# Norms between sublayers: ScalarE copies the residual stream, and halves of the rows go over two engines

## The chip, the core and the metric

The kernel runs on one core of one Trainium2 chip. The metric is the device time of one execution in microseconds (us), lower is better; shown is the median of three runs. The engines are TensorE (PE in the profile, its weight loads PEld), VectorE (DVE), ScalarE (ACT), GpSimd (POOL) and SyncE (SP), which issues nearly all DMAs. Each works through its own queue in order and meets the others by semaphores.

## The reference

A residual stream `x` of 128 rows by 512 columns (float32) goes through eight sublayers. Each is fed the layer norm of the stream, without gain or offset, and its result is added to the stream:

```python
def _layernorm(x, axis=-1, eps=1e-05):
    m = jnp.mean(x, axis=axis, keepdims=True)
    v = jnp.var(x, axis=axis, keepdims=True)
    return (x - m) / jnp.sqrt(v + eps)
...
x = x + _L0_gnn_ref(_layernorm(x, axis=-1), edge_index, L0_gnn_W, L0_gnn_a)
...
x = x + _L3_gnn_ref(_layernorm(x, axis=-1), edge_index, L3_gnn_W1, L3_gnn_b1, ...)
x = x + _L3_ffn_ref(_layernorm(x, axis=-1)[None], L3_ffn_router_w, L3_ffn_router_b, ...)[0]
```

The sublayers, numbered from 0 as their norms are: 0 graph attention over the edges, 1 grouped-query attention with a routed choice of weights, 2 a graph layer with linear attention (performer), 3 a product-key memory (it picks the best 16 of 256 sums for each row and head), 4 attention over the edges (exphormer), 5 eight transformer experts behind a gate, 6 three graph convolutions, 7 eight LSTM-like experts behind a router.

## The kernel before

Everything stays in on-chip memory, one row of the stream to a partition; weights come in by DMA ahead of use or, for the experts, as soon as the order of the experts is known. Every engine has one hand-written queue, and a step waits on a named semaphore's count; the order of the work is this writing, no planner is at work. Semaphores are named in `sig(...)` and waited for in `at(name, value)`. On VectorE, `settle()` drains the engine's own queue before a result is read again. `ps` is the accumulator memory that TensorE writes, eight banks of 512 columns.

A norm takes these steps; k is its number.

- The sums. At norms 2, 3, 4, 5 and 7, TensorE adds the residual stream and the sublayer's result in the accumulator memory, in two halves of 256 columns (norms 2, 4, 7) or four quarters of 128 (norms 3, 5), each signalled by `residual_summed`. At norms 0, 1 and 6 the stream lies in `x` already.
- Statistics on VectorE: `residual_norm` (L1907 to L1924) takes bn_stats of each part and aggregates; `layer_norm` (L1880) does it from `x` and serves norms 0 and 6; `layer_norm_routed` (L1891) serves norm 1, where the centred rows are written first because sublayer 1's choice needs them.
- GpSimd: `layer_norm_rstd` (L659 to L661) raises the variance to the power -1/2, `ln_rstd`.
- Rows on VectorE: two instructions, one for each half, write `y`, each signalled by `y_ready` (L1888, L1902, L1920). In `residual_norm` two copies from the accumulator memory to `x` follow (L1923), the second signalled by `x_updated`.
- TensorE: `layer_norm_transpose` (L1086 to L1093) waits for a half of `y` and transposes its two chunks of 128 columns into bank 7 or 6, signalled by `y_transposed`.
- ScalarE: `layer_norm_t` (L755 to L760) copies both halves of the transposed rows to `y_t`; the second copy is signalled by `y_t_ready`.
- TensorE waits for `y_t_ready` and `x_updated` and begins the sublayer's first product over the four chunks of `y_t`: mostly `project_t` (L1104 to L1109), four chunks summed for each output block; in sublayer 5 the gate's scores (L1663), in 6 the first convolution (L1721), in 7 the router's scores in bank 6 (L1829).

Ahead of a norm's transposes TensorE runs `keep_clock` (L1080 to L1084), products of the identity that nobody reads: 7 or 9 of them, 26 ahead of norm 6.

Behind norm 0 VectorE turns the edges to floats (L1985 to L1987) and makes the two one-hot tables (L1990) from which TensorE counts edges (L1197), and then copies attention terms (L1996). Behind norm 2 it spreads `y_t` into `x1_t`; behind norm 6 it adds a bias to `x` (L2509). GpSimd waits for `y_ready` of norm 5 before it adds `y` to expert rows (L722, L715).

Of the kernel before, what the change touches and what calls it, by code (L numbers as in the profile page):

```python
# [22 lines left out]
ALU = mybir.AluOpType  # L23
# [10 lines left out]
SUBLAYERS = 8  # L34

# [135 lines left out]
def build(nc, A, out):  # L171
# [14 lines left out]
    with ctx:  # L186
# [452 lines left out]
        def _(pool):  # L639
# [82 lines left out]
            pool.wait_ge(*at("y_ready", 12))  # L722
# [27 lines left out]
        def _(act):  # L750
# [58 lines left out]

            layer_norm_t(2)  # L810
# [35 lines left out]

            layer_norm_t(3)
# [30 lines left out]

            layer_norm_t(4)
# [9 lines left out]

            layer_norm_t(5)  # L890
# [114 lines left out]

            layer_norm_t(7)
# [69 lines left out]
        def _(pe):  # L1076
# [9 lines left out]
            def layer_norm_transpose(k):  # L1086

                for half in range(2):
                    pe.wait_ge(*at("y_ready", 2 * k + half + 1))
# [3 lines left out]
                    last.then_inc(sig("y_transposed"), 1)  # L1093
# [84 lines left out]
            pe.wait_ge(*at("y_t_ready", 1))  # L1178
            gat_w = slot("l0_W").rearrange("p (m c n) -> p m c n", m=CH, c=CH)
            pe.wait_ge(*at("gat_w_first_landed", 16))  # L1180
            for m in range(CH):
                if m == 2:
                    weights("l0_W")
                for c in range(CH):
                    last = pe.matmul(ps[:, m // 2, m % 2 * P:(m % 2 + 1) * P], gat_w[:, m, c, :], y_t[:, c, :],  # L1185
# [60 lines left out]
            pe.wait_ge(*at("y_t_ready", 2))  # L1246
# [36 lines left out]
            pe.wait_ge(*at("y_t_ready", 3))  # L1283
# [3 lines left out]
            for c in range(CH):  # L1287
                for w, name in enumerate(("perf_wq", "perf_wk")):
# [93 lines left out]
            pe.wait_ge(*at("y_t_ready", 4))  # L1382
# [3 lines left out]
            project_t(0, y_t, matrix("peer_wq"), chunks=2).then_inc(sig("peer_q_projected"), 1)  # L1386
# [57 lines left out]
            pe.wait_ge(*at("y_t_ready", 5))  # L1444
            pe.wait_ge(*at("x_updated", 4))
            weights("exph_wq")
            project_t(0, y_t, matrix("exph_wq")).then_inc(sig("exph_q_projected"), 1)
# [32 lines left out]
            pe.wait_ge(*at("y_t_ready", 6))  # L1480
# [181 lines left out]
            for c in range(CH):  # L1662
# [1058 lines left out]
```

## Time and profile before

| what | value |
|---|---|
| timed runs | 450.26, 448.14, 447.12 us; median 448.14 |
| profiled execution, span | 449.3 us (the page gives no time of its own beside the span) |
| TensorE busy | 412.4 us, 92% |
| VectorE busy | 214.4 us, 48% |
| ScalarE busy | 120.0 us, 27% |
| GpSimd busy | 35.0 us, 8% |
| mean granted TensorE clock | 0.981 |
| HBM read | 103.82 MB, 232 GB/s over the span |

The profile is of one execution, from its first to its last instruction, the span. Start times are us from the span's start, single durations us or ns. A group `out<-in` names what an instruction writes and reads; L1084 is a line of the kernel, and a line can be that of a helper, so that one line serves all norms. One float32 product of 128 by 128 by 128 appears as two records. TensorE's share of busy time includes `keep_clock`. The granted clock of 1.00 is 2.4 GHz, 0.50 is 1.2 GHz.

### The profile page before, as it was taken

How to read it: one execution, taken by the hardware profiler on the slowest of the kernel's cores; microseconds unless marked ns; L12 is line 12 of the kernel's file. 1: busy time of each engine (PE TensorE's matmuls, PEld its weight loads, DVE VectorE, ACT ScalarE, POOL GpSimd, SP SyncE). 2: the span in 40 equal slices, each digit the busy share in tenths (PEclk: the TensorE clock that was granted, in tenths of full speed). 3: DMA queues.
4: the chain of work that ended last, by engine and by line, in shares of the span. 5: the costliest groups of instructions: out<-in, count | busy, mean ns of one | idle time of the engine just before them, and what ended most of it. 6: DMA issues, size and time to landing. Idle time of an engine off the chain costs nothing.

```text
span 449.3 us, 7597 instructions
## 1 busy us (share of the span) xinstructions
PE 412.4 (92%) x2819; PEld 308.1 (69%) x2819; DVE 214.4 (48%) x631; ACT 120.0 (27%) x347; POOL 35.0 (8%) x68
## 2 busy tenths in 40 slices
PE   7998999994748989999998999999999999999996
PEld 6698655883247878797784668756778896394492
DVE  6744464457994254462754527557442631111102
ACT  2322313303220102251531325442111332222121
POOL 4000010011232001001000010002010000000000
PEclk9999999998699999999999899999999999999999
DMA  8999579222002200899999999336300299999900
GB/s 274 402 422 338 223 292 388 93 95 93 0 2 91 97 0 3 338 395 423 418 295 304 355 423 288 90 117 274 131 0 0 85 427 421 419 422 421 415 12 24
DMA packets 19631, 104.57 MB, mean 233 GB/s; under 512 B 3550, under 2 KB 5470, under 8 KB 7946
## 3 DMA queue, kind: packets, MB, share of 16 engines
q1 hardware_dynamic: 19306, 104.07, 60.9%
q8 instruction: 22, 0.36, 0.3%
q14 instruction: 15, 0.12, 0.1%
q10 hardware_dynamic: 288, 0.02, 0.0%
HBM read 103.82 MB, written 0.26 MB: 232 GB/s over the span
## 4 chain that ended last, share of the span: by engine, by line
PE 64%; DVE 15%; issue 7%; DMA 6%; ACT 3%; POOL 2%; DVEq 1%; SPq 1%; POOLq 0%; ACTq 0%
PE ps L1108 12%; PE ps L1096 8%; PE ps L1770 6%; PE ps L1510 5%; DMA dense<-in_l_w 5%; PE ps L1490 3%; PE ps L1499 3%; PE ps L1593 2%; PE ps L1084 2%; PE ps L1252 2%; PE ps L1092 1%; DMA ew<-in_l_wq 1%; PE ps L1185 1%; PE ps L1835 1%; PE ps L1289 1%
## 5 line engine op out<-in xcount | busy, mean ns | idle before, releaser
L1084 PE MATMUL ps<-ident 128*128 128x128 f32 x372 | 48.4, 284 | 2.7 <-POOL ident L647 2.7
L1084 PEld LDWEIGHTS ps<-ident 128*128 128x128 f32 x372 | 46.0, 199 | 5.1 <-POOL ident L647 2.7
L1108 PEld LDWEIGHTS ps<-y_t,ew 128*128 128x128 f32 x352 | 39.9, 192 | 1.7 <-issue 1.7
L1108 PE MATMUL ps<-y_t,ew 128*128 128x128 f32 x352 | 40.2, 275 | 0.0
L1096 PE MATMUL ps<-ew,y_t 128*128 128x512 f32 x72 | 32.7, 597 | 0.0
L1510 PE MATMUL ps<-y_t,ew 128*128 128x128 f32 x224 | 27.5, 277 | 0.0
L1510 PEld LDWEIGHTS ps<-y_t,ew 128*128 128x128 f32 x224 | 26.1, 192 | 0.8 <-issue 0.7
L768 ACT ACTIVATE prob_store<-ps,nmax_s 128x128 f32<-128x128 f32 x56 | 19.7, 384 | 14.6 <-DVE nmax_s L1957 14.6
L1096 PEld LDWEIGHTS ps<-ew,y_t 128*128 128x128 f32 x72 | 13.0, 190 | 13.5 <-issue 13.3
L758 ACT COPY y_t<-ps 128x256 f32<-128x256 f32 x16 | 5.7, 373 | 61.5 <-PE ps L1092 61.1
L2561 DVE SCALAR_TENSOR_TENSOR t<-prob_store 128x512 f32<-128x512 f32 x6 | 4.2, 692 | 36.4 <-ACT prob_store L1018 20.4
L720 POOL TENSOR_TENSOR ln_rstd<-ln_mv,minus_half 128x1 f32<-128x1 f32 x12 | 6.6, 547 | 133.3 <-DVE ln_mv L2321 133.3
L1499 PE MATMUL ps<-y_t,ew 128*128 128x128 f32 x128 | 15.7, 278 | 0.2 <-DMA ew<-in_l_wq 0.2
L1499 PEld LDWEIGHTS ps<-y_t,ew 128*128 128x128 f32 x128 | 14.9, 192 | 0.8 <-DMA ew<-in_l_wq 0.4
L1593 PE MATMUL ps<-ew,ctx_t 128*128 128x256 f32 x64 | 14.6, 381 | 0.3 <-ACT ctx_t L915 0.3
L1408 PE MATMUL ps<-dense,eq_t 128*8 128x512 f32 x8 | 6.4, 968 | 8.1 <-ACT big L866 8.1
L1593 PEld LDWEIGHTS ps<-ew,ctx_t 128*128 128x128 f32 x64 | 11.8, 190 | 1.9 <-ACT ctx_t L915 0.5
L768 ACT ACTIVATION_READ_ACCUMULATOR prob_store<-ps,nmax_s 128x1 f32 x56 | 12.5, 224 | 0.0
L1108 PE MATMUL ps<-y_t,dense 128*128 128x128 f32 x96 | 11.2, 277 | 0.9 <-ACT y_t L758 0.9
L1108 PEld LDWEIGHTS ps<-y_t,dense 128*128 128x128 f32 x96 | 10.9, 192 | 1.4 <-ACT y_t L758 1.4
L1096 PE MATMUL ps<-ew,x_t 128*128 128x512 f32 x24 | 11.1, 596 | 0.0
L1955 DVE TENSOR_REDUCE nmax<-ps 128x4 f32<-128x512 f32 x14 | 9.6, 686 | 2.5 <-PE ps L1119 2.3
(514 smaller groups left out, 751.0 us busy)
## 6 DMA issues: line engine op xcount, KB each, us to landing
ew<-in_l_w SPq DMA_DIRECT2D x20, 1024.0 KB, 21.8
dense<-in_l_w SPq DMA_DIRECT2D x12, 1024.0 KB, 21.2
ew<-in_l_wv SPq DMA_DIRECT2D x8, 1024.0 KB, 13.8
ew<-in_l_wk SPq DMA_DIRECT2D x7, 1024.0 KB, 16.3
ew<-in_l_wq SPq DMA_DIRECT2D x6, 1024.0 KB, 12.0
erows<-in_l_rows SPq DMA_DIRECT2D x4, 1280.0 KB, 12.5
ew<-in_l_wo SPq DMA_DIRECT2D x5, 1024.0 KB, 14.8
ew<-in_gqa_wq SPq DMA_DIRECT2D x3, 1024.0 KB, 10.9
```

What stands on the lines that cost most here:

```text
L720: pool.tensor_tensor(ln_rstd[:], ln_mv[:, 1:2], minus_half[:, 0:1], ALU.pow).then_inc(sig("l2_rstd_ready"), 1)
L768: last = nc.scalar.activation(prob[:, s, :], ps[:, 3 + a, g * P:(g + 1) * P], ACT.Exp, bias=nmax_s[:, s:s + 1], scale=scale, accum_out=rsu ...
L1084: pe.matmul(ps[:, b, 3 * P:4 * P], ident[:], ident[:], start=True, stop=True)
L1096: return pe.matmul(bank(b), in_t[:, c, :], w[:, c, :], start=(c == 0), stop=(c == CH - 1))
L1108: last = pe.matmul(ps[:, b, m * n:(m + 1) * n], w[:, c, (first + m) * P:(first + m + 1) * P], in_t[:, c, 0:n], start=(c == 0), stop=(c == ...
L1252: last = pe.matmul(ps[:, b, m * P:(m + 1) * P], w[:, m, c, :], y_t[:, c, :], start=(c == 0), stop=(c == CH - 1))
L1490: last = pe.matmul(ps[r, b, 0:columns.stop - columns.start], in_t[:, c, r], w_of[:, c, columns], start=(c == 0 and not started), stop=(c = ...
L1499: last = pe.matmul(ps[:, 0, m * P:(m + 1) * P], l2_w("q", p)[:, c, m * P:(m + 1) * P], y_t[:, c, :], start=(c == 0), stop=(c == CH - 1))
L1510: last = pe.matmul(ps[:, 1, m * P:(m + 1) * P], l2_w("k", p)[:, c, m * P:(m + 1) * P], y_t[:, c, :], start=(c == 0), stop=(c == CH - 1))
L1593: last = pe.matmul(ps[:, 5 + half, 0:D // 2], ctx_t[:, c, :], l2_w("o", L2_STEPS[t][0])[:, c, columns], start=(c == 0), stop=(c == CH - 1))
L1770: last = pe.matmul(ps[cols_of, b, :], in_t[:, c, cols_of], w_of[:, c, :], start=(c == 0 and not started), stop=(c == CH - 1))
L1955: dve.tensor_reduce(nmax[:, s], bank_chunks(3 + a), AX.X, ALU.max, negate=True)
```

## The change

The norms 0 and 2 to 7 (all but 1) are split by halves over two engines, and the first product waits by halves.

- ScalarE, no longer VectorE, copies the residual stream from the accumulator memory to `x` (`residual_copies`), each half as soon as VectorE has signalled its statistics (`residual_counted`). The two copies signal `x_copied` and `x_updated`.
- VectorE's `split_norm` subtracts the mean from the left half of `x` without waiting for `ln_rstd` (`y_centred`), and then makes the right half as before, but from `x`. ScalarE multiplies the left half by `ln_rstd` in place.
- The transposed left half is copied by ScalarE, the right one by VectorE (`second_half_t`, which stands right behind the norm in VectorE's queue). At norm 1 ScalarE copies both.
- TensorE waits for the first half of `y_t` ahead of chunk 0 of the first product and for the second ahead of chunk 2 (`normalised_chunk`).
- The semaphores `y_ready`, `y_transposed` and `y_t_ready` become one for each half. In sublayer 7 the router's scores and counts go to bank 5 and the transposed gates to bank 6, in exchange, since VectorE may still be reading bank 6.

The diff, cut: the same edits at other norms are left out.

```diff
+NORMS_OF_ROWS = tuple(range(SUBLAYERS))
+
+SPLIT_NORMS = tuple(k for k in NORMS_OF_ROWS if k != 1)
+
+RESIDUAL_NORMS = (2, 3, 4, 5, 7)
...
-            pool.wait_ge(*at("y_ready", 12))
+            pool.wait_ge(*at("y_ready0", 6))
+            pool.wait_ge(*at("y_ready1", 6))
...
             def layer_norm_t(k):
-                for half in range(2):
-                    act.wait_ge(*at("y_transposed", 2 * k + half + 1))
-                    last = nc.scalar.copy(y_t[:, 2 * half:2 * half + 2, :].rearrange("p c n -> p (c n)"),
-                                          ps[:, 7 - half, 0:2 * P])
-                last.then_inc(sig("y_t_ready"), 1)
+                n = NORMS_OF_ROWS.index(k) + 1
+                if k in SPLIT_NORMS:
+                    act.wait_ge(*at("y_centred", SPLIT_NORMS.index(k) + 1))
+                    act.wait_ge(*at("ln_rstd_ready", k + 1))
+                    nc.scalar.mul(y[:, 0:D // 2], y[:, 0:D // 2], ln_rstd[:]).then_inc(sig("y_ready0"), 1)
+                for half in range(1 if k in SPLIT_NORMS else 2):
+                    act.wait_ge(*at(f"y_transposed{half}", n))
+                    nc.scalar.copy(y_t[:, 2 * half:2 * half + 2, :].rearrange("p c n -> p (c n)"), ps[:, 7 - half, 0:2 * P]) \
+                        .then_inc(sig(f"y_t_ready{half}"), 1)
+
+            def residual_copies(summed, parts, halves):
+
+                for half, src in enumerate(halves):
+                    act.wait_ge(*at("residual_counted", summed + parts * (half + 1) // 2))
+                    out_half = x[:, half * D // 2:(half + 1) * D // 2]
+                    nc.scalar.copy(out_half if parts == 2 else out_half.rearrange("p (b n) -> p b n", b=2), src) \
+                        .then_inc(sig(("x_copied", "x_updated")[half]), 1)
...
+            residual_copies(0, 2, residual_halves((2, 3)))
             layer_norm_t(2)
...
+            residual_copies(2, 4, [ps[:, 0:2, 0:P], ps[:, 2:5:2, 0:P]])
             layer_norm_t(3)
...
             def layer_norm_transpose(k):
 
                 for half in range(2):
-                    pe.wait_ge(*at("y_ready", 2 * k + half + 1))
+                    pe.wait_ge(*at(f"y_ready{half}", NORMS_OF_ROWS.index(k) + 1))
                     for c in range(2):
                         f = (2 * half + c) * P
                         last = pe.transpose(ps[:, 7 - half, c * P:(c + 1) * P], y[:, f:f + P], ident[:])
-                    last.then_inc(sig("y_transposed"), 1)
+                    last.then_inc(sig(f"y_transposed{half}"), 1)
+
+            def normalised_chunk(k, c):
+
+                if c % 2 == 0:
+                    pe.wait_ge(*at(f"y_t_ready{c // 2}", NORMS_OF_ROWS.index(k) + 1))
...
-            def project_t(b, in_t, w, chunks=CH, first=0, n=P):
+            def project_t(b, in_t, w, chunks=CH, first=0, n=P, norm=None):
 
                 for m in range(chunks):
                     for c in range(CH):
+                        if norm is not None and m == 0:
+                            normalised_chunk(norm, c)
...
-            pe.wait_ge(*at("y_t_ready", 4))
             pe.wait_ge(*at("x_updated", 3))
             weights("peer_wq")
 
-            project_t(0, y_t, matrix("peer_wq"), chunks=2).then_inc(sig("peer_q_projected"), 1)
+            project_t(0, y_t, matrix("peer_wq"), chunks=2, norm=3).then_inc(sig("peer_q_projected"), 1)
...
-                last = pe.matmul(ps[:, 6, 0:E], y_t[:, c, :], router_w[:, c, :], start=(c == 0), stop=(c == CH - 1))
+                normalised_chunk(7, c)
+                last = pe.matmul(ps[:, 5, 0:E], y_t[:, c, :], router_w[:, c, :], start=(c == 0), stop=(c == CH - 1))
...
+            def split_norm(k):
+
+                left, right = slice(0, D // 2), slice(D // 2, D)
+                settle()
+                if k in RESIDUAL_NORMS:
+                    dve.wait_ge(*at("x_copied", RESIDUAL_NORMS.index(k) + 1))
+                dve.tensor_scalar(y[:, left], x[:, left], ln_mv[:, 0:1], None, ALU.subtract).then_inc(sig("y_centred"), 1)
+                if k in RESIDUAL_NORMS:
+                    dve.wait_ge(*at("x_updated", k))
+                dve.wait_ge(*at("ln_rstd_ready", k + 1))
+                dve.tensor_scalar(y[:, right], x[:, right], ln_mv[:, 0:1], ln_rstd[:], ALU.subtract, ALU.mult) \
+                    .then_inc(sig("y_ready1"), 1)
+
+            def second_half_t(k):
+                dve.wait_ge(*at("y_transposed1", NORMS_OF_ROWS.index(k) + 1))
+                dve.tensor_copy(y_t[:, 2:4, :].rearrange("p c n -> p (c n)"), ps[:, 6, 0:2 * P]).then_inc(sig("y_t_ready1"), 1)
...
             def layer_norm(k):
                 settle()
                 dve.bn_stats(ln_st[:, 0:6], x[:])
                 settle()
                 dve.bn_aggr(ln_mv[:], ln_st[:]).then_inc(sig("ln_var_ready"), 1)
+                split_norm(k)
...
-            def residual_norm(k, summed, parts, halves):
+            def residual_norm(k, summed, parts):
 
                 stats = half_st if len(parts) == 2 else part_st
                 for n, part in enumerate(parts):
                     dve.wait_ge(*at("residual_summed", summed + n + 1))
-                    dve.bn_stats(stats[:, 6 * n:6 * n + 6], part)
+                    dve.bn_stats(stats[:, 6 * n:6 * n + 6], part).then_inc(sig("residual_counted"), 1)
                 settle()
                 dve.bn_aggr(ln_mv[:], stats[:]).then_inc(sig("ln_var_ready"), 1)
-                settle()
-                dve.wait_ge(*at("ln_rstd_ready", k + 1))
-                shaped = lambda tile, half, src: tile[:, half * D // 2:(half + 1) * D // 2] if len(src.shape) == 2 else \
-                    tile[:, half * D // 2:(half + 1) * D // 2].rearrange("p (b n) -> p b n", b=2)
-                for half, src in enumerate(halves):
-                    dve.tensor_scalar(shaped(y, half, src), src, ln_mv[:, 0:1], ln_rstd[:], ALU.subtract, ALU.mult) \
-                        .then_inc(sig("y_ready"), 1)
-                for half, src in enumerate(halves):
-                    last = dve.tensor_copy(shaped(x, half, src), src)
-                last.then_inc(sig("x_updated"), 1)
+                split_norm(k)
...
             layer_norm(0)
+            second_half_t(0)
...
-            residual_norm(2, 0, residual_halves((2, 3)), residual_halves((2, 3)))
-
-            dve.wait_ge(*at("y_t_ready", 3))
+            residual_norm(2, 0, residual_halves((2, 3)))
+            second_half_t(2)
+
+            dve.wait_ge(*at("y_t_ready0", 3))
+            settle()
```

## Rows read from the trace of the kernel before

**Rows 1.** The page's chain that ended last: shares of the span by engine.

```profile
PE 64%; DVE 15%; issue 7%; DMA 6%; ACT 3%; POOL 2%; DVEq 1%; SPq 1%; POOLq 0%; ACTq 0%
```

**Rows 2.** Chain of waits in order of time, norm 4 and before: start, us, what.

```profile
137.51 1.79 PE ps L1084 x16
...
139.98 1.58 PE ps L1436 x6
...
141.58 0.86 DVE half_st L1912 x2
...
142.82 0.59 POOL ln_rstd L661
...
143.43 0.56 DVE y L1920
...
144.03 0.44 PE ps L1092 x2
...
144.49 0.45 PE ps L1092 x2
...
144.96 0.38 ACT y_t L758
```

**Rows 3.** Timeline of norm 4: start, us, engine, line, operation; idle time and releaser in brackets.

```profile
144.34 0.75 DVE L1923 COPY x<-ps 128x256 f32<-128x256 f32 x2
...
144.51 0.82 ACT L758 COPY y_t<-ps 128x256 f32<-128x256 f32 x2 [9.45 <-PE ps L1092]
...
145.38 3.84 PE L1108 MATMUL ps<-y_t,dense 128*128 128x128 f32 x32 [0.46 <-ACT y_t L758]
```

**Rows 4.** Chain of waits in order of time, behind norm 5.

```profile
180.24 4.83 DMA ew<-in_l_wq
```

**Rows 5.** Groups by shape: form and count, busy us, mean ns, idle before.

```profile
L866 ACT ACTIVATE big<-big,negbest 128x256 f32<-128x256 f32 x8 | 4.1, 508 | 0.3
...
L786 ACT ACTIVATE t<-ctxv,small 128x512 f32<-128x512 f32 x1 | 0.7, 722 | 2.8 <-DVE small L2032 2.8
...
L1923 DVE COPY x<-ps 128x256 f32<-128x256 f32 x10 | 3.7, 414 | 0.0
...
L1888 DVE TENSOR_SCALAR y<-x,ln_mv,ln_rstd 128x256 f32<-128x256 f32 x4 | 1.5, 417 | 1.8 <-POOL ln_rstd L661 1.8
...
L1902 DVE TENSOR_SCALAR y<-t,ln_rstd 128x256 f32<-128x256 f32 x2 | 0.6, 350 | 0.1
```

**Rows 6.** Timeline of norm 6.

```profile
330.60 0.69 ACT L758 COPY y_t<-ps 128x256 f32<-128x256 f32 x2 [6.20 <-PE ps L1092]
...
331.34 1.99 PE L1721 MATMUL ps<-dense,y_t 128*128 128x256 f32 x8 [0.46 <-ACT y_t L758]
```

**Rows 7.** Timeline of norm 1.

```profile
29.23 0.55 POOL L661 TENSOR_TENSOR ln_rstd<-ln_mv,minus_half 128x1 f32<-128x1 f32 x1 [23.54 <-DVE ln_mv L1896]
29.25 0.49 DVE L1898 TENSOR_SCALAR t<-x,ln_mv 128x512 f32<-128x512 f32 x1
```

**Rows 8.** Timeline of norm 0 and of the edge tables.

```profile
6.38 0.17 DVE L1985 CAST src_f<-src_i 128x17 f32<-128x17 int32 x1
...
6.67 0.89 PE L1092 MATMUL ps<-ident,y 128*128 128x128 f32 x4
...
7.34 0.65 ACT L758 COPY y_t<-ps 128x256 f32<-128x256 f32 x2 [4.33 <-PE ps L1092]
...
9.17 2.42 DVE L1990 TENSOR_TENSOR ew<-iota_f,dst_f 128x2176 bf16<-128x2176 f32 x1
...
13.03 0.28 DVE L1996 COPY gat_l<-ps 8x128 f32<-8x128 f32 x1 [1.44 <-PE ps L1193]
```

**Rows 9.** Timeline of TensorE alone, end of the product-key stage.

```profile
133.42 1.94 PE L1429 MATMUL ps<-x_t,prob_store 128*128 128x128 f32 x8 [5.19 <-POOL x_t L691]
```

**Rows 10.** Stretches: busy us of PE, PEld, DVE, ACT, POOL, then granted clock, DMA share, GB/s.

```profile
134.00:136.00 2.00, 2.00 (x9) 1.83 (x8) 1.90 (x8) 0.71 (x2) 0.60 (x1) 0.50 0.00 0
...
138.00:140.00 2.00, 1.77 (x17) 1.58 (x15) 0.37 (x2) 0.00 (x0) 0.00 (x0) 1.00 0.00 0
```

More of the change, by code:

```diff
@@ L887, in _ @@
             nc.scalar.copy(heads_v[:, :, 0:DH], bank_heads(2)).then_inc(sig("exph_v_ready"), 1)
+            residual_copies(8, 4, [ps[:, 1 + c:3 + c, 0:P] for c in (0, 2)])
             layer_norm_t(5)
@@ L1245, in _ @@
             keep_clock(1, times=9)
-            pe.wait_ge(*at("y_t_ready", 2))
+            for c in (0, 2):
+                normalised_chunk(1, c)
             def project_copied(b, w, copied):
@@ L1443, in _ @@
             layer_norm_transpose(4)
-            pe.wait_ge(*at("y_t_ready", 5))
             pe.wait_ge(*at("x_updated", 4))
             weights("exph_wq")
-            project_t(0, y_t, matrix("exph_wq")).then_inc(sig("exph_q_projected"), 1)
+            project_t(0, y_t, matrix("exph_wq"), norm=4).then_inc(sig("exph_q_projected"), 1)
             weights("exph_wk")
@@ L1718, in _ @@
                     for c in range(CH):
+                        if k == 0 and half == 0:
+                            normalised_chunk(6, c)
                         if k and half == 0 and c % 2 == 0:
@@ L1841, in _ @@
             pe.wait_ge(*at("lstm_tables_ready", LSTM_TABLES))
-            pe.matmul(ps[:, 6, 8:16], ones[:], mask8, start=True, stop=True)
-            pe.matmul(ps[:, 6, 16:24], upper, mask8, start=True, stop=True).then_inc(sig("router_counted"), 1)
+            pe.matmul(ps[:, 5, 8:16], ones[:], mask8, start=True, stop=True)
+            pe.matmul(ps[:, 5, 16:24], upper, mask8, start=True, stop=True).then_inc(sig("router_counted"), 1)
             first_gate((2, 3)).then_inc(sig("l3_gates_projected"), 1)
@@ L1846, in _ @@
             pe.wait_ge(*at("lstm_gated_ready", 1))
-            pe.transpose(ps[0:E, 5, 0:P], gated[:], ident[:]).then_inc(sig("lstm_gated_transposed"), 1)
+            pe.transpose(ps[0:E, 6, 0:P], gated[:], ident[:]).then_inc(sig("lstm_gated_transposed"), 1)
             lstm_gates(0, (2,))
@@ L1884, in layer_norm @@
                 dve.bn_aggr(ln_mv[:], ln_st[:]).then_inc(sig("ln_var_ready"), 1)
-                settle()
-                dve.wait_ge(*at("ln_rstd_ready", k + 1))
-                for half in (slice(0, D // 2), slice(D // 2, D)):
-                    dve.tensor_scalar(y[:, half], x[:, half], ln_mv[:, 0:1], ln_rstd[:], ALU.subtract, ALU.mult) \
-                        .then_inc(sig("y_ready"), 1)
+                split_norm(k)
             def layer_norm_routed(k):
@@ L1900, in layer_norm_routed @@
                 dve.wait_ge(*at("ln_rstd_ready", k + 1))
-                for half in (slice(0, D // 2), slice(D // 2, D)):
-                    dve.tensor_scalar(y[:, half], t1[:, half], ln_rstd[:], None, ALU.mult).then_inc(sig("y_ready"), 1)
+                for n, half in enumerate((slice(0, D // 2), slice(D // 2, D))):
+                    dve.tensor_scalar(y[:, half], t1[:, half], ln_rstd[:], None, ALU.mult).then_inc(sig(f"y_ready{n}"), 1)
             def residual_halves(banks):
                 return [ps[:, b, 0:D // 2] for b in banks]
-            def residual_norm(k, summed, parts, halves):
+            def residual_norm(k, summed, parts):
                 stats = half_st if len(parts) == 2 else part_st
@@ L2172, in _ @@
             batch_norm(1, ctx_t, N2G, N2B)
-            residual_norm(3, 2, [ps[:, b, 0:P] for b in (0, 1, 2, 4)], [ps[:, 0:2, 0:P], ps[:, 2:5:2, 0:P]])
+            residual_norm(3, 2, [ps[:, b, 0:P] for b in (0, 1, 2, 4)])
+            second_half_t(3)
             dve.wait_ge(*at("peer_q_projected", 1))
@@ L2278, in _ @@
             batch_norm(2, ctx_t, BNG, BNB)
-            residual_norm(5, 8, [ps[:, 1 + c, 0:P] for c in range(CH)], [ps[:, 1 + c:3 + c, 0:P] for c in (0, 2)])
+            residual_norm(5, 8, [ps[:, 1 + c, 0:P] for c in range(CH)])
+            second_half_t(5)
             def top2():
@@ L2532, in _ @@
             dve.wait_ge(*at("router_counted", 1))
-            dve.scalar_tensor_tensor(keys8[:, 1:E], ps[:, 6, 9:16], 8.0, iota_f[:, 1:E], ALU.mult, ALU.subtract)
+            dve.scalar_tensor_tensor(keys8[:, 1:E], ps[:, 5, 9:16], 8.0, iota_f[:, 1:E], ALU.mult, ALU.subtract)
             settle()
```

29 lines of the change are left out of this document (16 added, 13 removed).

## Prediction

> **What bounds the kernel now.** I read the page's chain of waits first: TensorE holds 64% of it, VectorE 15%, ScalarE 3%, GpSimd 2% [rows 1]. So the kernel is one long chain that hops between engines, and what counts is the links that a norm between sublayers puts into it. The chain in order of time shows them for norm 4 [rows 2]: VectorE's statistics end at 142.44, GpSimd's power at 143.41, VectorE writes the first half of y until 143.99, TensorE transposes it from 144.03, and the second half only from 144.49, because VectorE brings it that much later; ScalarE's second copy ends at 145.34. The timeline of the same stretch has the first product at 145.38 [rows 3]: 1.97 us from the power's end to the product, in which TensorE has only four transposes. The same links, within 0.01 us, stand at five places, norms 2, 3, 4, 5 and 7. The timeline also shows what is not among them: VectorE's two copies of x end at 145.09, before y_t is there, and ScalarE had been idle for 9.45 us before its two copies.
>
> Time saved there is passed on. Behind norm 5 comes the order of the experts, and only that sends the load at 180.24, on which TensorE then waits until 185.07 [rows 4]: issue and landing move with the norm, they do not absorb it.
>
> **The change, part by part.** The sums are for the profiled execution: span 449.3, and the page gives no time around it, which I take as the same before and after. The timed runs have a median of 448.14 and a highest of 450.26, so the profile is an ordinary execution 0.3% above the median; I take the differences off the median.
>
> *Halves side by side, and a product that waits by halves (norms 2, 3, 4, 5, 7).* The path after the power becomes: ScalarE multiplies the centred left half by ln_rstd, TensorE transposes it, ScalarE copies it, the product starts. No row has a ScalarE multiply of 128x256 from SBUF with a per-row scale. It should not be under the plain 128x256 copy from PSUM, 0.38 [rows 2], nor over the 128x512 activation with a per-row operand at L786, 0.722 [rows 5]. The nearest row is L866, 128x256 from SBUF with a per-row operand, 0.508: I take 0.51. It starts at 143.43 as VectorE did and ends at 143.94, 0.05 before VectorE's half did (143.99). The first transpose moves to 143.98. ScalarE's first copy began 0.48 after it (144.51 against 144.03 [rows 2, 3]), so it runs from 144.46 to 144.84, and the product starts at 144.88 instead of 145.38. Gain 0.50, nearly all of it the 0.45 by which the second half used to trail. With the multiply's two ends: 0.63 and 0.29.
>
> The right half must not spoil it. VectorE's subtract-and-multiply from SBUF takes 0.417 (L1888 [rows 5]) and ends at 143.85, before ScalarE's, so the four transposes run in one piece. In norm 6, where the halves lay close, the second copy began 0.31 after the first (0.69 for both, 0.38 for one [rows 2, 6]). VectorE's copy of the second half, 0.414 (L1923), would run from 144.77 to 145.18 and let chunk 2 go at 145.22. Chunks 0 and 1 keep TensorE busy until then: 32 records take 3.84 [rows 3], 0.12 each, so their four take 0.48, until 145.36. Cover 0.14; without it the product loses only what is missing.
>
> *The copies of x.* Two of 0.38 on ScalarE, each behind the statistics of its half, beside the aggregation and the power: the second runs from 142.47 to 142.85, 0.56 before the power ends. Queued behind it on ScalarE is only this norm's own work. VectorE's centring of the left half, 0.350 (L1902), starts with the power at 142.82 and ends at 143.17, 0.24 ahead of it. I cost both at nothing; were a copy twice as long, the 0.56 would still hide it. VectorE loses its 0.75 of copies and gains nothing by that: behind them it waits for TensorE's products, in norm 2 for y_t itself.
>
> *A VectorE instruction beside the power.* Norm 1 shows that pair already [rows 7]: the power from 29.23 to 29.78, VectorE's centring of 128x512 from 29.25 to 29.74, and the power, at 0.55, is not longer than norm 4's 0.59 without company. Nothing again. The Trainium skill ("SBUF — State Buffer", Who interferes with whom) says that a VectorE instruction of this kind and a GpSimd one shut each other out for the whole instruction; norm 1's rows do not agree, but a rival below keeps it.
>
> *Norm 6.* x lies in SBUF there, and VectorE needed 0.41 for its first half; ScalarE's 0.51 is 0.10 later. The first copy ends 0.31 before the second did. Gain 0.21 of the wait that ended at 331.34 [rows 6]. The addition to x behind VectorE's new wait is wanted only in the third layer.
>
> *Norm 0, a loss.* VectorE now waits for the second transposes before it turns to the edges, and behind those TensorE waits for the one-hot tables [rows 8]. The transposes stand behind TensorE's fillers and start at 6.67 whatever the norm does; ScalarE's second copy began near 7.61, so VectorE's would run from 7.61 to 8.02, and the casts that began at 6.38 come 1.64 later. The tables ended at 11.59 (9.17 + 2.42) and will end at 13.23; the chain met VectorE at 13.03. So 0.20 is lost, plus 0.03 of start-up: 0.23. TensorE's own gain of 0.27 (one copy instead of two) is overtaken by that. The ends: a gain of 0.27 if the tables had the room, a loss of 1.64 if there were no slack.
>
> *The rest.* Norm 1 keeps its form. GpSimd's wait (both halves instead of a count of 12) guards residual rows off the path. SP's queue is untouched. Router scores in bank 5 instead of 6 are the same instructions.
>
> Sum: 5 x 0.50 + 0.21 - 0.23 = 2.48 us, so 448.14 - 2.48 = 445.7, and a span near 446.8. The multiply at 0.38 and norm 0 a gain of 0.27 make it 3.8 (444.3); the multiply at 0.722 makes it 1.2 (446.9), norm 0's worst end 1.1 (447.1).
>
> **Rivals.**
> *The second half is the late one.* VectorE's copy comes so late that TensorE gains nothing from its early chunks: the product in effect starts at 145.22, a gain of 0.16 each and none in norm 6, 5 x 0.16 - 0.23 = 0.57: 447.6. For it: a cover of only 0.14. Against it: the 0.48 of work is counted from rows, and a late half costs only the difference.
>
> *VectorE and GpSimd hold each other up.* The power begins when the centring ends (143.17 instead of 142.82), or the centring when the power ends; either puts 0.35 on five norms and on norm 6, 2.1 together: 447.8. For it no row speaks; against it norm 1. It is what the skill's rule named above would give.
>
> *The clock comes back too late: slower.* Near the end of the product-key stage TensorE has waited 5.19 us [rows 9]; the granted clock is then 0.50 (1.2 GHz) and from 138 on 1.00 (2.4 GHz) [rows 10]. Behind that the chain still runs 1.79 and 1.58 us on TensorE [rows 2]. Should the clock come back only after these, they double: 3.4 us more, 449.1, slower than before. It decides at 137.5. For it: the stage is entered over a microsecond earlier, and no row says what that does. Against it: the idle time ahead of it is the same.
>
> *The clock comes back sooner.* The eight records at 133.42 took 1.94 [rows 9] at the lower level; with the upper one 0.97 less, and about as much for what follows until 137.5: some 1.8 us, 443.9, and 442.5 with the good ends above.
>
> **How the numbers follow.** The forecast 0.62 (its own range 444.3 to 447.1), the late half 0.12, the mutual hold 0.07, the late clock 0.07, the early clock 0.12. A measurement of this kernel tells about 1% from no change, here 4.5 us: below 443.7, above 452.6. Faster by more needs the early clock and part of the good ends: 0.12 with the forecast's own tail. Slower by more needs the late clock and two more losses: 0.04. That leaves 0.84 within 1%. The range goes from 443.8 to 448.3: it holds the forecast, the late half, the hold and the early clock alone, and leaves out the late clock and the early one with more beside it.
>
> **What would show it.** In the profile of after: the product of norm 4 some 1.47 us after the power's end instead of 1.97, ScalarE's multiply near 0.51, VectorE's copy done before chunk 2 is due, the power still 0.55 to 0.59, the edge casts near 8.0 and the tables' end near 13.2, the granted clock around 137 as before. I am wrong if the product waits for VectorE, if the power grows, if ScalarE's multiply starts well after the power's end, or if the stages behind the norms do not keep their lengths.

## The result and the profile after

In the first set of runs the changed kernel takes 446.31 us (median of 12, 444.98 to 450.1) and the kernel before 449.81 beside it; the ratio is 0.9914, 95% interval 0.9892 to 0.9936. By the medians that is 3.5 us faster, by the ratio 3.9, somewhere between 2.9 and 4.9. A second set, below, gives 0.9941 (0.9900 to 0.9983), 2.7 us by the ratio. Both are under 1%. The forecast was 445.7, a gain of 2.5.

The profiled execution has a span of 445.1 us and was timed at 446.79, so about 1.7 us lie around the span. VectorE's busy time is 1.6 us less than before and ScalarE's 5.1 more. Its engines:

```profile
PE 408.7 (92%) x2819; PEld 308.4 (69%) x2819; DVE 212.8 (48%) x628; ACT 125.1 (28%) x357; POOL 35.2 (8%) x68
```

The timeline of the changed kernel: norm 0 and the edge tables (which answers to [rows 8]), the aggregation of norm 1, norm 4 (which answers to [rows 2, 3]), and norm 6's power and product (to [rows 6]). Columns are start, duration, engine, line, operation; in brackets the idle time before and what ended it.

```profile
6.59 0.60 PE L1119 MATMUL ps<-ident,y 128*128 128x128 f32 x4
...
7.01 0.37 ACT L770 COPY y_t<-ps 128x256 f32<-128x256 f32 x1 [0.69 <-PE ps L1119]
...
7.57 0.17 DVE L2025 CAST src_f<-src_i 128x17 f32<-128x17 int32 x1
...
10.36 2.42 DVE L2030 TENSOR_TENSOR ew<-iota_f,dst_f 128x2176 bf16<-128x2176 f32 x1
...
12.83 0.95 PE L1232 MATMUL ps<-ew 128*128 128x128 bf16 x14 [0.38 <-DVE ew L2030]
...
28.36 0.20 DVE L1944 BATCH_NORM_AGGREGATE ln_mv<-ln_st 128x2 f32<-128x9 f32 x1
...
141.58 0.58 POOL L667 TENSOR_TENSOR ln_rstd<-ln_mv,minus_half 128x1 f32<-128x1 f32 x1 [7.26 <-DVE ln_mv L1962]
141.59 0.35 DVE L1921 TENSOR_SCALAR y<-x,ln_mv 128x256 f32<-128x256 f32 x1
...
142.26 0.51 ACT L767 ACTIVATE y<-y,ln_rstd 128x256 f32<-128x256 f32 x1 [0.67 <-POOL ln_rstd L667]
142.27 0.41 DVE L1925 TENSOR_SCALAR y<-x,ln_mv,ln_rstd 128x256 f32<-128x256 f32 x1 [0.32 <-POOL ln_rstd L667]
...
142.82 0.66 PE L1119 MATMUL ps<-ident,y 128*128 128x128 f32 x4 [0.54 <-ACT y L767]
...
143.29 0.37 ACT L770 COPY y_t<-ps 128x256 f32<-128x256 f32 x1 [0.53 <-PE ps L1119]
143.51 0.42 DVE L1930 COPY y_t<-ps 128x256 f32<-128x256 f32 x1 [0.82 <-PE ps L1119]
...
143.78 0.97 PEld L1142 LDWEIGHTS ps<-y_t,dense 128*128 128x128 f32 x8 [0.54 <-issue]
143.81 1.02 PE L1142 MATMUL ps<-y_t,dense 128*128 128x128 f32 x7 [0.34 <-ACT y_t L770]
...
325.33 0.55 POOL L667 TENSOR_TENSOR ln_rstd<-ln_mv,minus_half 128x1 f32<-128x1 f32 x1 [2.25 <-DVE ln_mv L1936]
...
327.53 1.75 PE L1756 MATMUL ps<-dense,y_t 128*128 128x256 f32 x7 [0.34 <-ACT y_t L770]
```

What to see: ScalarE's multiply, which no row of before had, takes 0.51 us as estimated. The four transposes run in one piece (0.66), the two copies side by side, and the product runs on without waiting for the second. The power is 0.58 long although VectorE's centring lies wholly beside it. But the chain has two cracks. The power ends at 142.16 and the multiply starts 0.10 later; ScalarE's copy ends at 143.66 and the product starts 0.15 later (the load of its weights is put down to "issue", that is, to nothing the profile shows). So the product comes 1.65 us after the power's end, against 1.97 before and a forecast of 1.47. The same holds in norms 2, 3, 5 and 7: 0.33 to 0.35 gained in each, and 0.11 in norm 6 (1.76 before, 1.65 after).

Aligning TensorE's records of the two profiles one by one, the changed kernel is ahead by 0.60 us at norm 1's power, 0.91 at norm 2's product, 1.57 at norm 4's, 1.90 at norm 5's, 3.65 at 249 us, and 4.17 at norm 7's product. Beside the norms there are two sources nobody forecast: 0.6 us before norm 2 and 1.6 us in the experts' stage, between 244 and 250 us. The experiments went after the cracks, the parts of the change, and these two.

### The profile page after: what moved, and what is told of

Same layout as the page of the kernel before. It is cut to its first block, busy times and chain, and to the rows that moved or that the text cites. A ratio compares the mean times of both kernels' runs of the same rounds, so it can differ in the third digit from the quotient of the medians.

```text
span 445.1 us, 7617 instructions
## 1 busy us (share of the span) xinstructions
PE 408.7 (92%) x2819; PEld 308.4 (69%) x2819; DVE 212.8 (48%) x628; ACT 125.1 (28%) x357; POOL 35.2 (8%) x68
## 4 chain that ended last, share of the span: by engine, by line
PE 45%; DMA 6%; issue 5%; DVE 3%; ACT 1%; SPq 1%; DVEq 0%; POOL 0%; POOLq 0%; ACTq 0%
PE ps L1142 9%; PE ps L1804 6%; PE ps L1128 6%; PE ps L1543 5%; DMA dense<-in_l_w 5%; PE ps L1523 3%; PE ps L1532 3%; PE ps L1626 2%; DMA ew<-in_l_wq 1%; PE ps L1870 1%; PE ps L1647 1%; PE ps L1162 1%; PE ps L1111 1%; PE ps L1634 1%; PE ps L1153 1%
## 5 line engine op out<-in xcount | busy, mean ns | idle before, releaser
L1111 PE MATMUL ps<-ident 128*128 128x128 f32 x372 | 50.0, 290 | 2.7 <-POOL ident L653 2.7
L1111 PEld LDWEIGHTS ps<-ident 128*128 128x128 f32 x372 | 47.8, 205 | 5.1 <-POOL ident L653 2.7
L778 ACT COPY x<-ps 128x256 f32<-128x256 f32 x10 | 3.7, 373 | 32.7 <-DVE part_st L1960 18.2
L1443 PE MATMUL ps<-dense,eq_t 128*8 128x512 f32 x8 | 4.9, 772 | 8.1 <-ACT big L890 8.1
```

What stands on the lines that cost most here:

```text
L1111: pe.matmul(ps[:, b, 3 * P:4 * P], ident[:], ident[:], start=True, stop=True)
L1443: last = pe.matmul(ps[0:E, 0, :], eq_t[:, c, :], matrix("gate_wk")[:, c, :], start=(c == 0), stop=(c == CH - 1))
```

## The experiments

**How to compare them.** Single runs of one kernel spread over as much as 5 us. Each timed run lists its span and its mean granted clock, and these go together: within the kernels of this study the span falls by 0.32 us for each 0.001 of mean clock (a straight line fitted by least squares over 197 runs). In the table the last column takes every kernel's mean span to a clock of 0.980 with that slope; the plus-minus is its standard error. The kernel before was run anew with each set of experiments; its three sets give 448.1, 448.0 and 448.0 at 0.980, so kernels of different sets may be compared.

| kernel | runs | mean span, us | mean clock | span at 0.980, us |
|---|---|---|---|---|
| before | 75 | 448.26 | 0.9792 | 448.01 ± 0.12 |
| changed, both sets | 21 | 445.15 | 0.9814 | 445.61 ± 0.25 |
| late_first | 12 | 445.41 | 0.9800 | 445.41 ± 0.33 |
| norm0_whole | 6 | 444.78 | 0.9820 | 445.43 ± 0.30 |
| halves_alone | 12 | 446.78 | 0.9798 | 446.72 ± 0.27 |
| joint | 12 | 447.94 | 0.9814 | 448.40 ± 0.34 |
| one_engine | 12 | 445.57 | 0.9802 | 445.62 ± 0.23 |
| one_engine_late | 12 | 445.96 | 0.9773 | 445.10 ± 0.15 |
| one_engine_best, both sets | 14 | 444.64 | 0.9805 | 444.80 ± 0.21 |
| split_best | 9 | 445.32 | 0.9798 | 445.25 ± 0.22 |
| before_drain | 12 | 448.58 | 0.9796 | 448.44 ± 0.14 |

At equal clock the change is worth 2.4 us (95%: 1.9 to 2.9).

**1. The order of waits (late_first).**

```diff
-                    act.wait_ge(*at("y_centred", SPLIT_NORMS.index(k) + 1))
                     act.wait_ge(*at("ln_rstd_ready", k + 1))
+                    act.wait_ge(*at("y_centred", SPLIT_NORMS.index(k) + 1))
...
             layer_norm_transpose(4)
+            pe.wait_ge(*at("y_t_ready0", 5))
             pe.wait_ge(*at("x_updated", 4))
```

> Edit: the changed kernel, where the wait that ends last is written first of those ahead of an instruction (ln_rstd ahead of y_centred on ScalarE and ahead of the x waits on VectorE, y_t_ready0 ahead of x_updated and the weights on TensorE). In the changed kernel the first product of a norm starts 1.64 us after the power's end, where 1.47 was forecast; 0.07 of the missing time lies between the power's end and ScalarE's multiply (0.10 instead of 0.03), 0.10 between ScalarE's copy and the product (0.14 instead of 0.04). Theory, order of the waits: the lags go back to about 0.04 and 0.05, the product comes 1.44 to 1.50 us after the power, and the kernel is 7 x 0.15 = about 1 us faster than the changed one. Rival, the lags belong to the engines and to two engines waiting on one semaphore: 1.64 as in the changed kernel, and the same time.

The timeline of late_first, norm 4:

```profile
142.65 0.58 POOL L667 TENSOR_TENSOR ln_rstd<-ln_mv,minus_half 128x1 f32<-128x1 f32 x1 [8.08 <-DVE ln_mv L1969]
...
143.26 0.51 ACT L767 ACTIVATE y<-y,ln_rstd 128x256 f32<-128x256 f32 x1 [0.60 <-POOL ln_rstd L667]
...
144.30 0.37 ACT L770 COPY y_t<-ps 128x256 f32<-128x256 f32 x1 [0.53 <-PE ps L1119]
...
144.72 0.52 PEld L1142 LDWEIGHTS ps<-y_t,dense 128*128 128x128 f32 x4 [0.48 <-ACT y_t L770]
144.72 0.60 PE L1142 MATMUL ps<-y_t,dense 128*128 128x128 f32 x3 [0.24 <-ACT y_t L770]
```

The multiply starts 0.03 after the power's end (143.23), the product 0.05 after the copy's (144.67): 1.49 us in all (1.49 to 1.50 in the five norms), where 1.47 was forecast. The weight load is now released by ScalarE, not by "issue". That settles the cracks: nothing but the order of the waits was changed, and in both places the lag is short when the wait that ends last is the first one written. In the time the 1 us does not show: 447.04 us, ratio to before 0.9919 (0.9886 to 0.9953), and 0.2 ± 0.4 under the changed kernel at equal clock. In this profile the start (norm 0's transposes took 1.06 us instead of 0.60) cost 0.54 and the product-key stage 0.84 more than in the changed kernel's, against 0.15 to 0.17 gained in each norm; for the other runs that was not shown.

**2. Norm 0 (norm0_whole).**

```diff
-SPLIT_NORMS = tuple(k for k in NORMS_OF_ROWS if k != 1)
+SPLIT_NORMS = tuple(k for k in NORMS_OF_ROWS if k > 1)
...
             layer_norm(0)
-            second_half_t(0)
```

> Edit: norm 0 alone goes back to rows by VectorE and transposed copies by ScalarE; its product still waits by halves. The prediction's step for norm 0: VectorE's wait for the second transposes moves the edge casts (7.57 in the changed kernel, 6.38 before) and the end of the one-hot tables (12.78 against 11.59), for which TensorE waits. If the tables bind TensorE, they end near 11.6 here, and the stages behind them start 0.2 to 0.4 us earlier than in the changed kernel. Rival: another load or VectorE's own next work ends last there, the tables move by 1.2 us and nothing behind them by more than 0.1.

The timeline of norm0_whole, tables and norm 1's aggregation:

```profile
9.18 2.42 DVE L2036 TENSOR_TENSOR ew<-iota_f,dst_f 128x2176 bf16<-128x2176 f32 x1
...
12.54 1.12 PE L1232 MATMUL ps<-ew 128*128 128x128 bf16 x17
...
28.57 0.20 DVE L1951 BATCH_NORM_AGGREGATE ln_mv<-ln_st 128x2 f32<-128x9 f32 x1 [0.49 <-issue]
```

The tables end at 11.60 and TensorE enters the edges at 12.54, with no wait for them, instead of 12.83 with a wait of 0.38. The loss in norm 0 is shown, 0.29. Yet at norm 1 this kernel is 0.2 behind the changed one: VectorE stands 0.49 us ahead of the aggregation, for nothing that the profile shows. The kernel before does the same, the changed one does not (28.36 above). In time the ratio to before is 0.9899 (0.9847 to 0.9951), and 0.2 ± 0.4 us under the changed kernel at equal clock. The timeline of the kernel before, norm 1:

```profile
28.96 0.20 DVE L1896 BATCH_NORM_AGGREGATE ln_mv<-ln_st 128x2 f32<-128x9 f32 x1 [0.49 <-issue]
```

**3. The wait by halves alone (halves_alone).** The semaphores by half and sublayer 7's exchanged banks come with it.

```diff
+            def normalised_chunk(k, c):
+                if c % 2 == 0:
+                    pe.wait_ge(*at(f"y_t_ready{c // 2}", NORMS_OF_ROWS.index(k) + 1))
...
-            pe.wait_ge(*at("y_t_ready", 5))
             pe.wait_ge(*at("x_updated", 4))
...
                     for c in range(CH):
+                        if norm is not None and m == 0:
+                            normalised_chunk(norm, c)
```

> Edit: the kernel before with the product's wait by halves alone; VectorE makes all rows and the copies of x, ScalarE both transposed copies, as before. The prediction put the 0.50 us of a norm down to the second half that trailed by 0.45, and so to the split over two engines and the wait together. If the wait is enough, the first product starts 1.52 to 1.62 us after the power's end (1.97 before, 1.64 in the changed kernel). Rival: the copies of x, which VectorE makes behind its rows, now end last (1.69 us after the power's end in the kernel before), and the product starts at 1.74 to 1.84: 0.13 to 0.23 of gain per norm in norms 2, 3, 4, 5 and 7, and 0.3 to 0.45 in norm 6, which has no such copy; in all 1.0 to 1.6 us faster than before.

The timeline of halves_alone, norm 4 (its power ends at 142.59):

```profile
143.54 0.74 DVE L1970 COPY x<-ps 128x256 f32<-128x256 f32 x2
...
143.70 0.83 ACT L770 COPY y_t<-ps 128x256 f32<-128x256 f32 x2 [9.45 <-PE ps L1114]
...
144.34 0.71 PE L1137 MATMUL ps<-y_t,dense 128*128 128x128 f32 x4 [0.22 <-DVE x L1970]
```

The rival holds: the product is released by VectorE's copy of x (ends 144.28), 1.75 us after the power. Norm 6, without such a copy, starts at 1.54, a gain of 0.22 and not the 0.3 to 0.45 expected. In time 0.9962 (0.9937 to 0.9988), 1.3 us at equal clock, as this rival gave (1.0 to 1.6). So the copies of x on ScalarE are no side matter: without them the wait by halves brings 0.23 in each of these norms, and with them, in the next experiment, 0.38 (there the rows are made from `x` too).

**4. No split over two engines (one_engine).**

```diff
-SPLIT_NORMS = tuple(k for k in NORMS_OF_ROWS if k != 1)
+SPLIT_NORMS = tuple(k for k in NORMS_OF_ROWS if k > 99)
...
-                dve.tensor_scalar(y[:, left], x[:, left], ln_mv[:, 0:1], None, ALU.subtract).then_inc(sig("y_centred"), 1)
...
+                for n, half in enumerate((slice(0, D // 2), slice(D // 2, D))):
+                    dve.tensor_scalar(y[:, half], x[:, half], ln_mv[:, 0:1], ln_rstd[:], ALU.subtract, ALU.mult) \
+                        .then_inc(sig(f"y_ready{n}"), 1)
...
-            second_half_t(4)
```

> Edit: the changed kernel without the split over two engines. ScalarE still copies x, and the product still waits by halves, but VectorE makes both row halves from x and ScalarE both transposed copies. Worked out from rows: 0.10 to VectorE's start behind three waits, 0.46 for the first half as in norm 6 before, 0.05 to the transpose, 0.48 to the copy, 0.37 for it, 0.14 to the product: 1.60 us after the power's end against 1.64 in the changed kernel. So by this theory the split of the rows and of the transposed copies gives nothing of the gain, and without it norm 0 loses nothing: the same time as the changed kernel or up to 0.5 us less. Rival, the split is what pays: the second half trails again, chunk 2 waits for it, and each norm is 0.2 to 0.45 later, 1.2 to 2.7 us in all.

The timeline of one_engine, norm 4:

```profile
142.63 0.58 POOL L667 TENSOR_TENSOR ln_rstd<-ln_mv,minus_half 128x1 f32<-128x1 f32 x1 [8.04 <-DVE ln_mv L1960]
...
143.35 0.74 DVE L1923 TENSOR_SCALAR y<-x,ln_mv,ln_rstd 128x256 f32<-128x256 f32 x2 [0.80 <-POOL ln_rstd L667]
...
144.29 0.70 ACT L770 COPY y_t<-ps 128x256 f32<-128x256 f32 x2 [1.65 <-PE ps L1119]
...
144.81 1.46 PE L1142 MATMUL ps<-y_t,dense 128*128 128x128 f32 x11 [0.22 <-ACT y_t L770]
```

Measured 1.60 us from the power's end to the product in norm 4 (143.21 to 144.81), as worked out; ratio 0.9930 (0.9900 to 0.9961), and at equal clock the changed kernel's time within 0.0 ± 0.3 us. VectorE, which now reads `x` and not the accumulator memory, brings the second half 0.33 after the first instead of 0.46, and the first two chunks of the product cover that. The split over two engines gives nothing of the gain that these runs could show.

**5. The second half awaited (joint).**

```diff
-                if c % 2 == 0:
-                    pe.wait_ge(*at(f"y_t_ready{c // 2}", NORMS_OF_ROWS.index(k) + 1))
+                if c == 0:
+                    pe.wait_ge(*at("y_t_ready0", NORMS_OF_ROWS.index(k) + 1))
+                    pe.wait_ge(*at("y_t_ready1", NORMS_OF_ROWS.index(k) + 1))
```

> Edit: the changed kernel, where TensorE waits for both halves of y_t before the first product; rows, copies of x and transposed copies stay on two engines. VectorE's copy of the second half ends 0.27 us after ScalarE's of the first, so the product should start 0.22 to 0.28 us later in each of seven norms, 1.86 to 1.92 us after the power's end against 1.64, and 1.97 in the kernel before: some 1.7 us slower than the changed kernel. So of a norm's 0.33 the halves on two engines without the wait by halves keep 0.05 to 0.11. Rival, the wait by halves gives little, as the second half is due right behind: less than 0.1 per norm.

The timeline of joint, norm 4 (its power ends at 142.52):

```profile
143.65 0.37 ACT L770 COPY y_t<-ps 128x256 f32<-128x256 f32 x1 [0.53 <-PE ps L1119]
143.87 0.42 DVE L1931 COPY y_t<-ps 128x256 f32<-128x256 f32 x1 [0.83 <-PE ps L1119]
...
144.44 0.68 PE L1143 MATMUL ps<-y_t,dense 128*128 128x128 f32 x4 [0.61 <-DVE y_t L1931]
```

The product is released by VectorE, 1.92 us after the power: 0.05 of the gain is left. In time the ratio to before is 0.9992 (0.9964 to 1.0020). The whole change without the wait by halves gains nothing that can be measured. At equal clock it is 2.8 ± 0.4 us slower than the changed kernel, where 1.7 was expected; the 0.27 us that each of norms 2 to 7 loses in the trace do not account for all of that.

**6. The stall in norm 1 (before_drain).**

```diff
             dve.wait_ge(*at("x_landed", 16))
+            settle()
             layer_norm(0)
```

> Edit: the kernel before with one more drain on VectorE ahead of norm 0, where VectorE stands idle; nothing else. In norm 1 of the kernel before VectorE waits 0.49 us for nothing that the profile shows between the statistics and the aggregation; the aggregation is the 64th of its instructions there. In the changed kernel the norm has one instruction more ahead of it, the 64th is the drain beside the statistics, and the gap is gone, which gives 0.41. Theory, the stall belongs to the place in VectorE's order of instructions: here too it falls on that drain, the aggregation of norm 1 starts 0.41 us earlier than in the kernel before, and the stages behind follow. The other gaps of that kind move by one instruction as well (448th and 832nd). Rival, it belongs to what the instructions wait for: the gap stays at 0.49.

The timeline of before_drain, norm 1 and the experts:

```profile
28.57 0.20 DVE L1896 BATCH_NORM_AGGREGATE ln_mv<-ln_st 128x2 f32<-128x9 f32 x1
...
217.92 0.75 DVE L2370 SCALAR_TENSOR_TENSOR acc<-t,rg,acc 128x512 f32<-128x512 f32 x1 [0.45 <-issue]
```

One drain moves the stall: the aggregation comes 0.39 earlier. But the instruction that is now the 576th catches one of its own, 0.45, where in the kernel before a semaphore instruction stood in that place and hid it; by 219.3 us TensorE has lost the 0.36 again. The time is that of before, 0.9999 (0.9970 to 1.0027); that it lies 0.4 higher at equal clock, two standard errors, is explained by nothing in the trace. The theory that the stall belongs to the place in the order holds; the gain does not last.

**7. and 8. Without the split, late wait first (one_engine_late), and with the drain (one_engine_best).** The first edit, the drain, is in one_engine_best alone.

```diff
+            settle()
             layer_norm(0)
...
+                dve.wait_ge(*at("ln_rstd_ready", k + 1))
                 if k in RESIDUAL_NORMS:
                     dve.wait_ge(*at("x_copied", RESIDUAL_NORMS.index(k) + 1))
                     dve.wait_ge(*at("x_updated", k))
-                dve.wait_ge(*at("ln_rstd_ready", k + 1))
```

> Edit: as one_engine (ScalarE copies x, product by halves, VectorE alone makes the rows, ScalarE alone the transposed copies), with the wait that ends last written first on VectorE and TensorE. one_engine has 1.60 us from the power's end to the product; 0.11 of it ahead of VectorE's rows and 0.15 ahead of the product. Theory: these go to 0.03 and 0.05, the product comes 1.43 to 1.47 us after the power's end, 0.17 to 0.21 per norm better than the changed kernel, in all 1.0 to 1.3 us, and 0.3 more from norm 0's tables; VectorE's stall in norm 1 (0.41) is back, as in one_engine. Rival, the order of waits changes nothing: 1.60.

> Edit: one_engine_late with one more drain on VectorE ahead of norm 0. Theory, the stall belongs to the place in the order: the aggregation of norm 1 comes 0.41 us earlier than in one_engine_late, the rest as there; the best version of the study, some 1.5 to 2 us faster than the changed kernel and 4.5 to 5.5 us faster than the kernel before. Rival: the gap stays, and both run alike.

The timeline of one_engine_best, norm 4:

```profile
141.12 0.58 POOL L667 TENSOR_TENSOR ln_rstd<-ln_mv,minus_half 128x1 f32<-128x1 f32 x1 [6.97 <-DVE ln_mv L1967]
...
141.74 0.73 DVE L1930 TENSOR_SCALAR y<-x,ln_mv,ln_rstd 128x256 f32<-128x256 f32 x2 [0.70 <-POOL ln_rstd L667]
...
142.68 0.70 ACT L770 COPY y_t<-ps 128x256 f32<-128x256 f32 x2 [1.55 <-PE ps L1119]
...
143.10 0.71 PE L1142 MATMUL ps<-y_t,dense 128*128 128x128 f32 x4
```

1.40 us from the power's end (141.70), in one_engine_late the same. Ratios to before: 0.9945 (0.9915 to 0.9976) for one_engine_late and 0.9893 (0.9848 to 0.9937) for one_engine_best. At equal clock one_engine_late is 0.5 ± 0.3 us under the changed kernel, where the expectation adds up to 0.9 to 1.2 (1.0 to 1.3 from the norms and 0.3 from the tables, less 0.41 for the stall). In one_engine_best the stall in norm 1 is gone from the trace, as expected; in time the two differ by 0.3 ± 0.3, which does not show it.

**9. and 10. The best version again, and its split form (one_engine_best_2, split_best).** The second is late_first, norm0_whole and the drain together.

> one_engine_best unaltered, run again beside the changed kernel on the same chip. Its first set gave 445.6 against 450.4 for the kernel before. Theory: 1.41 us from the power's end to the product against 1.64, no late tables and no stall in norm 1: 1.2 to 2 us faster than the changed kernel in the same set. Rival: the norms gain that and the clock takes it back, the difference is under 0.5.

> Edit: the changed kernel with the late wait written first (late_first), norm 0 whole (norm0_whole) and one drain more on VectorE ahead of norm 0. Against one_engine_best it differs in the split alone: rows and transposed copies of norms 2 to 7 on two engines. Theory, ScalarE's multiply from SBUF is slower than VectorE's, so the split costs: 1.49 us from the power's end to the product against 1.41 in one_engine_best, 6 x 0.08 = 0.5 us slower in all. Rival: the shorter second half shows in the products behind, and both are equal.

447.07 us, ratio 0.9919 (0.9889 to 0.9949), and 446.84, 0.9928 (0.9899 to 0.9957), beside 447.83 for the changed kernel in the same set. 1.49 against 1.40 us in the norms, as expected; the difference in time is too small for these runs. Over both sets and at equal clock one_engine_best lies 0.8 ± 0.3 us under the changed kernel and 3.2 under the kernel before: the lowest of the study, by less than the 1.2 to 2 hoped for.

**11. and 12. Both kernels again (after_again, before_again).**

> The changed kernel unaltered, a second set of runs and a second profile. Two things are open. First, the trace comparison gives the norms 1.8 us of gain, while the runs gave 3.6 to 3.9; among runs of equal mean granted clock the difference is some 2.5. Second, the kernel before has a stretch of granted clock 0.50 near 246 us of its span, which alone makes 1.6 of the difference between the two profiles, and the changed kernel has none. If the stretch is chance, the changed kernel's runs here have a lower mean clock than the first set (0.982) and lie near 446.5 to 447.5; if the change itself moved it, they stay at 0.982 and near 446.3.

> The kernel before unaltered, for a second profile. If the stretch of granted clock 0.50 near 246 us is a part of the kernel before, it is here too; if it is chance, it is missing or lies elsewhere, and the experts' stage is then as long as in the changed kernel.

447.83 us, 0.9941 (0.9900 to 0.9983), mean clock 0.981 against 0.982 in the first set: later than either expectation. Stretches (as in [rows 10], for TensorE alone: the stretch, its length, TensorE's busy time in it with the records, granted clock, DMA share, GB/s) of the kernel before, its second profile, the changed kernel, and its second profile:

```profile
246.00:248.00 2.00, 2.00 (x10) 0.54 1.04 319
...
350.00:352.00 2.00, 1.94 (x17) 1.00 0.03 8
```

```profile
246.00:248.00 2.00, 2.00 (x26) 1.00 1.03 396
...
350.00:352.00 2.00, 2.00 (x12) 0.55 0.03 8
```

```profile
246.00:248.00 2.00, 2.00 (x16) 1.00 1.03 251
...
348.00:350.00 2.00, 2.00 (x20) 1.00 0.00 0
```

```profile
246.00:248.00 2.00, 2.00 (x18) 1.00 1.00 249
...
348.00:350.00 2.00, 2.00 (x12) 0.50 0.00 0
```

The stretch at the lower level (1.2 GHz) near 246 us is missing from the second profile of the kernel before, which has one near 351 instead; the changed kernel has none in one execution and one near 349 in the other. It belongs to the execution, not to the change: 1.6 of the 4.17 us between the two first profiles are chance. Whether the changed kernel's higher mean clock (0.9814 against 0.9792, some three standard errors) is chance too stays open; at the slope above it is worth 0.7 us, and the gain before that is taken out is 3.1.

## Why the prediction was right, and where its steps were not

The time and the size of the gain came out: forecast 2.48, measured 2.4 (1.9 to 2.9) at equal clock. The terms fit less well than the sum, and part of the fit is luck. Norms 2 to 7 gave 1.8 where 2.7 was forecast, and 0.41 of that came back from a stall in norm 1 of which the prediction knew nothing. The time, 446.31 against 445.7, was counted from 448.14, the median of three runs; the twelve runs of the same kernel have 449.81, so here a low start and a larger gain in this set made up for each other.

*Five norms, 0.50 each: mis-sized, measured 0.33 to 0.35.* The durations held: multiply 0.51, centring 0.35, right half 0.41, the copy 0.47 after the first transpose. What failed is the step "It starts at 143.43 as VectorE did ... and the product starts at 144.88": it carried over the lags of the kernel before, 0.02 and 0.04, to instructions with more waits ahead of them, in another order. late_first changes the order alone and puts the missing 0.16 back. The reason given for the gain, the second half that trailed by 0.45, was right as to the wait by halves (joint loses it all) and wrong as to the two engines (one_engine keeps it all).

*Copies of x at nothing: right as to their cost, too small as to their worth.* The prediction said that VectorE "gains nothing by that". halves_alone shows what hung on it: x would have been the last thing the product waits for.

*Norm 6, 0.21: measured 0.11,* again by the lags.

*Norm 0, a loss of 0.23: right in place and near in size,* 0.29 against the same kernel with norm 0 whole (norm0_whole), though the casts came at 7.57 and the tables' end at 12.78 instead of 13.23, since the transposes took 0.60 instead of 0.89 ([rows 8]). In late_first, where they took 1.06, the tables end at 13.31. One reading behind the term was wrong: the 13.03 at which "the chain met VectorE" is a copy that waits for TensorE. TensorE itself entered the edges at 12.92, so that tables ending at 13.23 would have cost above 0.3. The timeline of the kernel before, edges:

```profile
12.92 1.12 PE L1197 MATMUL ps<-ew 128*128 128x128 bf16 x17
```

Between the two first profiles no loss is seen, 12.83 against 12.92, because the transposes ended 0.37 earlier in the changed kernel (7.19 against 7.56); counted from their end, the edges come 0.28 later.

*Norm 1, "keeps its form": wrong by 0.41 in the good direction.* The change put one more instruction of VectorE ahead of it, and a stall moved under the statistics.

So 5 x 0.34 + 0.11 - 0.29 + 0.41 = 1.93; the 0.5 up to 2.4 lies within the uncertainty, and no run shows an owner for it. The start, told at the end, is a candidate.

*The rivals.* The late second half: no; the product never waits for VectorE's copy. The mutual hold: no; the power is 0.54 to 0.58 in the six norms with the centring beside it, and the rule of the Trainium skill ("SBUF — State Buffer", Who interferes with whom) is not what this pair does here. The two clock rivals at the product-key stage: neither; the changed kernel also has 0.50 in 134 to 136 and 1.00 in 138 to 140, and its lead grows from 1.24 us at norm 3's product to 1.57 at norm 4's, which is that norm's own 0.33. That the clock decides over a microsecond was right, that it would do so at one place and by the change was not: it does so at several, by the execution.

## What to carry to other kernels

A product that starts on the first half needs everything else it waits for to be early too: look for the next latest wait (here the copy of x) before counting the gain. Where several waits stand ahead of one instruction, write the one that ends last first. And before splitting work over two engines, ask whether starting on the first half doesn't already hide the second.

## What the runs showed of the hardware that was not expected

*Order of waits.* The same semaphore ended the wait, yet ScalarE's instruction started 0.10 us after it with the late wait written second and 0.03 with it first; TensorE's product 0.15 and 0.05.

*A stall by place in the order of instructions.* Counting VectorE's instructions as the trace has them, its idle times ahead of instructions without a wait of their own, 0.24 to 0.49 us each and put down to "issue", sit at the 64th, 448th, 576th, 704th or 832nd instruction, or one behind, in all of these kernels: 64 and steps of 128. (The other idle times under "issue", of 0.16, 1.1 and 4.2 us, stand ahead of the same instructions in every kernel.) At the 192nd and 320th none is seen in any kernel. That a drain in such a place hides the stall is shown in norm 1; what hides the others was not looked into. The Trainium skill ("Runtime: NRT & Kernel Launch", Instruction fetch mechanics) says that a sequencer gets its instructions in blocks and that crossing from one to the next is mostly hidden; no run here shows that these stalls are that. The rows show that it depends on the instruction in that place whether the stall is seen, and that one instruction more or less moves 0.4 us.

*The start.* Norm 0's four transposes, behind the same fillers, took 0.89 and 1.06 us in the two profiles of the kernel before, 0.60 and 0.66 in those of the changed kernel, and 0.60 to 1.06 in the other kernels; the profile's granted clock reads 1.00 there in all of them. One and the same kernel took 1.06 (one_engine_best) and 0.60 (one_engine_best_2), so two single profiles can differ by another half microsecond without any change. Whether all of it is chance stays open: the kernel before and before_drain (0.93) took 0.89 or more in all three of their profiles.
